# Dividing attention by its row sums behind the weighted sum of values instead of ahead of the transposes

## What is computed

```python
q = _rms_norm(q, g_q)
k = _rms_norm(k, g_k)
logits = jnp.einsum('bhqd,bhkd->bhqk', q, k) * d ** (-0.5)
attn = jax.nn.softmax(logits, axis=-1)
o = jnp.einsum('bhqk,bhkd->bhqd', attn, v)
o = jnp.swapaxes(o, 1, 2).reshape(b, n, dim)
return o + o @ W_out
```

## Time and profile before

| what | us |
|---|---|
| median of 3 runs | 3099.62 |
| the three runs | 3105.89, 3098.64, 3099.62 |
| the profiled execution, device time | 3095.6 |
| its span, first to last instruction | 3093.5 |
| start of batch 1 / batch 2 in it (first sum of squares on TensorE) | 186.03 / 292.83 |
| start of the last network, behind batch 7 | 961.5 |
| first matmul of layer 1 | 1039.5 |

### The profile page before, as it was taken

How to read it: one execution, slowest core, us unless ns; L and a number is a source line. 1 busy time by engine, 2 the same in 40 slices (tenths; PEclk the granted TensorE clock), 3 DMA queues, 4 the chain that set the end, 5 groups by cost and what they waited for, 6 DMA issues and landing times.

```text
span 3093.5 us, 130035 instructions
## 1 busy us (share of the span) xinstructions
PE 2879.0 (93%) x47184; PEld 2502.9 (81%) x47184; DVE 1746.1 (56%) x6459; ACT 1065.8 (34%) x4862; POOL 1284.5 (42%) x3409
## 2 busy tenths in 40 slices
PE   6899999999999556899999999999999999999998
PEld 4368777767778455899999899899899899899987
DVE  1636644644642444566666666666666666666654
ACT  1122332543442122333333333333333333333322
POOL 0000000100110466666666566566566566656600
PEclk7589999999999655799999999999999999999999
DMA  4613312532532000244444444444344444444466
GB/s 146 201 38 103 99 58 67 183 95 88 184 101 75 25 0 0 71 128 130 135 129 126 127 131 128 125 130 127 119 139 127 123 130 128 119 135 129 129 215 203
DMA packets 137146, 359.18 MB, mean 116 GB/s; under 512 B 16016, under 2 KB 24848, under 8 KB 136592
## 3 DMA queue, kind: packets, MB, share of 16 engines
q1 hardware_dynamic: 136336, 353.72, 37.7%
q10 hardware_dynamic: 672, 3.67, 0.3%
HBM read 322.85 MB, written 34.47 MB: 116 GB/s over the span
## 4 chain that ended last, share of the span: by engine, by line
PE 60%; DVE 3%; issue 2%; ACT 1%; DMA 0%; DVEq 0%; POOL 0%; ACTq 0%; SPq 0%; POOLq 0%
PE pscan L1019 13%; PE pscan L1015 13%; PE pg L946 11%; PE pd L972 11%; PE pu L946 11%; ACT th L869 1%; DVE state L1176 1%; DVE qraw L1176 0%; PE prouter L1029 0%; PE prouter L1037 0%; DMA wgu<-w_split 0%; PE pd L1044 0%; DVE pscan L1162 0%; DVEq L1175 0%; DVE th L1159 0%
## 5 line engine op out<-in xcount | busy, mean ns | idle before, releaser
L1015 PEld LDWEIGHTS pscan<-th,clo 128*128 128x128 f16 x16384 | 555.8, 97 | 143.5 <-ACT th L869 123.0
L1015 PE MATMUL pscan<-th,clo 128*128 128x8 f16 x16384 | 564.3, 167 | 109.8 <-ACT th L869 109.8
L1019 PE MATMUL pscan<-th,chi 128*128 128x16 f16 x16384 | 561.5, 170 | 3.0 <-DVE th L1159 2.3
L1019 PEld LDWEIGHTS pscan<-th,chi 128*128 128x128 f16 x16384 | 486.8, 97 | 4.5 <-DVE th L1159 4.5
L946 PE MATMUL pg<-qh,wgu 128*128 128x256 f16 x3168 | 430.5, 275 | 16.7 <-issue 15.8
L972 PE MATMUL pd<-hg,wd 128*128 128x256 f16 x3168 | 429.8, 275 | 2.2 <-DMA wd<-w_split 2.2
L946 PE MATMUL pu<-qh,wgu 128*128 128x256 f16 x3168 | 426.3, 274 | 0.0
L869 ACT ACTIVATE th<-state 128x32 f16<-128x32 f32 x768 | 175.9, 229 | 719.3 <-DVE state L1176 719.1
L1176 DVE TENSOR_REDUCE state<-pscan 128x32 f32<-128x96 f32 x768 | 197.4, 257 | 265.0 <-PE pscan L1019 259.7
L946 PEld LDWEIGHTS pg<-qh,wgu 128*128 128x128 f16 x3168 | 295.5, 98 | 55.9 <-issue 17.2
L946 PEld LDWEIGHTS pu<-qh,wgu 128*128 128x128 f16 x3168 | 294.1, 98 | 34.0
(11 more groups left out here) (164 smaller groups left out, 4286.8 us busy)
## 6 DMA issues: line engine op xcount, KB each, us to landing
wgu<-w_split SPq DMA_DIRECT2D x264, 512.0 KB, 3.6
wd<-w_split SPq DMA_DIRECT2D x264, 384.0 KB, 3.1
part_in<-in_w_tiles SPq DMA_DIRECT2D x120, 256.0 KB, 3.0
w_split<-part_out SPq DMA_DIRECT2D x99, 256.0 KB, 2.8
late<-in_w_tiles SPq DMA_DIRECT2D x78, 256.0 KB, 3.0
w_split<-late SPq DMA_DIRECT2D x33, 128.0 KB, 3.3
hid<-in_up_q SPq DMA_DIRECT2D x8, 512.0 KB, 4.0
hid<-in_up_s SPq DMA_DIRECT2D x16, 256.0 KB, 5.5
```

What stands on the lines that cost most here:

```text
L1015: mm(pscan[:, 0, m * B:(m + 1) * B], clo[:, k, m * P:(m + 1) * P], th[:, k, 0, :], start=(m == 0 and k == 0), stop=False, skip_group_check ...
L1019: ins = mm(pscan[:, 0:2, m * B:(m + 1) * B], chi[:, k, m * P:(m + 1) * P], th[:, k], start=False, stop=(k == NC - 1), skip_group_check=True)
```

## The change

The exponentials are transposed as they are. `normed` and the accumulated sums go away. In `weighted(c)` eight matmuls more, ahead of the eight with the values, multiply the same transposed exponentials `prT` with a 128x32 block of ones; they leave the sum of each query on the 32 rows of its head, in columns 256 to 511 of the same bank. On VectorE `inverse(c - 1)` takes the reciprocal of these 128x256 sums and `gathered(c - 1)` multiplies it into the weighted sums; both stand inside quad c, behind `turned(h + 1)` and `turned(h + 2)`, and those of quad 3 behind the loop. ScalarE no longer copies `Ob`.

```diff
@@ scalar
                         ins = act.activation(pr[:, h % HPC, qc, :], X[h % HPC][:, qc * T:(qc + 1) * T], ACT.Exp,
-                                             bias=nmax[:, h % HPC, qc:qc + 1], accum_out=psum_e[:, h, qc:qc + 1])
+                                             bias=nmax[:, h % HPC, qc:qc + 1])
-                def gathered(c):
-                    act.wait_ge(S["p_pv"], b * NC + c + 1)
-                    act.activation(oT[:, c, :], Ob[c % 2][:, 0:T], ACT.Copy).then_inc(S["a_oT"], 1)
@@ tensor
                 def transposed(h):
-                    pe.wait_ge(S["d_pn"], b * HEADS + h + 1)
+                    pe.wait_ge(S["a_exp"], b * HEADS + h + 1)
@@ tensor, weighted(c)
                     if c >= 2:
-                        pe.wait_ge(S["a_oT"], b * NC + c - 1)
+                        pe.wait_ge(S["d_oT"], b * NC + c - 1)
+                    for kc in range(2):
+                        for j in range(HPC):
+                            mm(Ob[c % 2][DH * j:DH * (j + 1), T:2 * T], ones[:, 0:DH], prT[:, j, kc, :], start=(kc == 0), stop=(kc == 1))
@@ vector
-                def normed(h):
-                    dve.wait_ge(S["a_exp"], b * HEADS + h + 1)
-                    dve.reciprocal(rinv[:, h, :], psum_e[:, h, :]).then_inc(S["d_rinv"], 1)
-                    dve.wait_ge(S["d_rinv"], b * HEADS + h + 1)
-                    for qc in range(2):
-                        ins = dve.tensor_scalar(pr[:, h % HPC, qc, :], pr[:, h % HPC, qc, :], rinv[:, h, qc:qc + 1], None, ALU.mult)
-                    ins.then_inc(S["d_pn"], 1)
+                def inverse(c):
+                    dve.wait_ge(S["p_pv"], b * NC + c + 1)
+                    dve.reciprocal(rinv, Ob[c % 2][:, T:2 * T]).then_inc(S["d_rinv"], 1)
+                def gathered(c):
+                    dve.wait_ge(S["d_rinv"], b * NC + c + 1)
+                    dve.tensor_tensor(oT[:, c, :], Ob[c % 2][:, 0:T], rinv, ALU.mult).then_inc(S["d_oT"], 1)
@@ vector, the loop over quads
                     row_max(h)
                     row_max(h + 1)
-                    normed(h)
                     row_max(h + 2)
-                    normed(h + 1)
                     turned(h)
                     row_max(h + 3)
-                    normed(h + 2)
                     turned(h + 1)
-                    normed(h + 3)
+                    if c:
+                        inverse(c - 1)
                     turned(h + 2)
+                    if c:
+                        gathered(c - 1)
                     turned(h + 3)
                     if ffn and c == NC - 1:
                         second(b - 1, 0)
+                inverse(NC - 1)
+                gathered(NC - 1)
```

More of the change, by code:

```diff
@@ L87, in layer0 @@
         nmax = sb("nmax", [P, HPC, 2])
-        psum_e = sb("psum_e", [P, HEADS, 2])
-        rinv = sb("rinv", [P, HEADS, 2])
+        rinv = rs[:, 0, :]
         late = sb("late", [P, N + H0 + NC * T])
@@ L108, in layer0 @@
                  "p_nrm p_qk p_hr p_v p_s p_t p_pv p_wo p_up p_dn "
-                 "a_sqx a_rstd a_sq a_hr a_v a_exp a_oT a_up "
-                 "d_xn d_qk d_max d_rinv d_pn d_pt d_x1 d_x2 "
+                 "a_sqx a_rstd a_sq a_hr a_v a_exp d_oT a_up "
+                 "d_xn d_qk d_max d_rinv d_pt d_x1 d_x2 "
                  "chain achain seq plseq "
@@ L315, in batch @@
                     exps(HPC * c + 1)
-                    if c:
-                        gathered(c - 1)
                     relus(ffn_quad[c][0:2])
@@ L322, in batch @@
                     relus(ffn_quad[c][3:])
-                gathered(NC - 1)
             batch(0, False)
@@ L466, in batch @@
                     pe.wait_ge(S["wo_in"], 16)
-                pe.wait_ge(S["a_oT"], b * NC + NC)
+                pe.wait_ge(S["d_oT"], b * NC + NC)
                 for m in range(NC):
@@ L591, in batch @@
                     if i == 0:
-                        dve.wait_ge(S["a_oT"], b * NC + NC)
+                        dve.wait_ge(S["d_oT"], b * NC + NC)
                     dve.tensor_tensor(x1[:, 2 * i:2 * i + 2, :].rearrange("p a t -> p (a t)"), Rb[i][:], oT[:, 2 * i:2 * i + 2, :].rearrange("p a t -> p (a t)"), ALU.add).then_inc(S["d_x1"], 1)
```

## The result

| | before | changed |
|---|---|---|
| median of 20 runs each, us | 3099.14 | 3104.72 |
| lowest and highest | 3092.95, 3105.89 | 3101.43, 3112.13 |
| profiled execution, device time | 3095.6 | 3109.9 |
| its span | 3093.5 | 3107.9 |

The ratio of changed to before is 1.002, with a 95% interval of 1.0014 to 1.0026: **slower by 5.6 us (4.3 to 8.1)**. The borders of the stages are good to 0.4 us.

A forecast was written before the change was run, and what follows sets the result against it. TensorE bounds batches 1 to 3, with waits in batches 4 to 7 and a half-clock ring in batch 0. 17.0 + 3.1 + 7.2 = 27.3 us, so about 3127 us, 0.9% slower; range 3108 to 3140.

The forecast's parts named there:

- one group of sums at full clock: Eight added matmuls with ones on TensorE: 0.86 us a group at full clock, 1.72 at half.
- the reciprocal: VectorE's 128x256 reciprocal from PSUM: 1.82 us, between bounds of 0.41 and 2.45.
- batches 1 to 3, a wait: TensorE waits 0.74 us for VectorE's row at the ends of quads 1, 2 and 3, 2.2 us a batch.
- batches 1 to 3, all: Sums of 3.44 us plus waits of 2.2 us lengthen each batch by 5.66 us: 17.0 us for three.
- batches 4 to 7: Sums outside quad 1 cost 10.3 us, waits for `normed` outside it give back 7.2: +3.1 us.
- batch 0, quad 0: First quad of batch 0, without sums: no gain or loss counted.
- batch 0, quads 1 and 2: `weighted` lies on the ring between `scores` and `lora`; sums at half clock cost 2 x 1.72 = 3.4 us.
- batch 0, quad 3 and the end: Nothing hides the last reciprocal and product; the projection begins 3.8 us later, at 181.0 instead of 177.19.
- the ReLU wait that stays: TensorE's wait for a ReLU behind the store ring, once in each of batches 4 to 7, remains at 2 us or more.
- What ScalarE loses ... and what VectorE loses gives nothing beyond the waits named: ScalarE's 256 accumulator reads and 32 copies, and VectorE's removed work, save nothing more: neither engine is waited for elsewhere.
- both give about the same time, so the ring and the ReLU stay: Quad 1, batches 4 to 7: `part_low` comes when it did, so the ReLU wait hides `weighted(0)`'s sum, costing nothing.
- the third: Rival, chance 0.09: store ring opens, ReLU wait goes, batches 4 to 7 14.1 us faster; 3110 us, narrow reciprocal 3100.

The follow-up runs named there:

- the first pair: Single profiled executions of the kernel before and the changed kernel, 3095.6 and 3109.9 us.
- the means: Averages of batches 4 to 7 over several traces: attention of the kernel before 457.9 us, of the changed kernel 455.7 us.
- the kernels of the first group: Here, kernel before with the eight sum matmuls added, result unused: in every quad 3121.37 us, in batch 0 only 3097.28 us.
- the new form: Attention as in the changed kernel, in all or some batches; the changed kernel took 3104.72 us, run again 3110.29.
- the ReLU first: Last ReLUs ahead of the store-waiting high parts in quad 1 of batches 4 to 7: kernel before 3081.43 us, changed kernel 3095.07 us.
- its later half: Changed kernel's attention in batches 1 to 7, that of the kernel before in batch 0: 3116.72 us, again 3113.34 us.
- the early reciprocal behind batch 0: Changed kernel with reciprocal and product ahead of a quad's first copy in batches 1 to 7 alone: 3104.67 us, ratio 1.0011.
- the early reciprocal everywhere: Changed kernel with reciprocal and product ahead of a quad's first copy in all batches: 3107.07 us, ratio 1.0025.
- the copy: Changed kernel with a plain copy of the 128x256 sums in place of the reciprocal: 3103.74 us, ratio 1.0006.
- the kernel with the sums alone: Kernel before with the eight matmuls with ones added in each quad, result unused: 3121.37 us, ratio 1.007.
- the frame: Both attention forms in one program with two unused tensors: changed kernel's form everywhere 3107.48 us, form of the kernel before everywhere 3101.98 us.
- The halves run apart: Kernel before with the changed attention in batch 0 alone, 3098.34 us; in batches 1 to 7 alone, 3116.72 and again 3113.34 us.
- the old form: Attention as in the kernel before, in all or some batches; the kernel before took 3099.14 us.

## The prediction against the runs, step by step

| step | forecast | measured |
|---|---|---|
| one group of sums at full clock | 0.86 | 0.87 |
| the reciprocal | 1.82 | 1.75 |
| batches 1 to 3, a wait | 3 x 0.74 a batch | 2 x 0.44 a batch |
| batches 1 to 3, all | +17.0 | +13.2 |
| batches 4 to 7 | +3.1 | +3.3 in the first pair, -2.2 in the means |
| batch 0, quad 0 | 0 | -1.7 in the first pair |
| batch 0, quads 1 and 2 | +3.4 | -2.6 in the first pair |
| batch 0, quad 3 and the end | +3.8 | +2.5 in the first pair |
| all | +27.3 | +5.6 |

**Right.** The sums at full clock, the reciprocal, the untouched layer 1, the ReLU wait that stays, and that no engine is spared anything that counts in batches 1 to 3.

**The waits for the reciprocal** were right in kind and too long. The rows above have 8.57 us for VectorE where I had 8.88, of which 0.16 is that the next instruction starts 1.66 us after a reciprocal begins and 0.08 the same for the product. A wait of 0.44 us stands only in quads 2 and 3; in quad 1 TensorE's own stretch is 0.49 us longer by a ReLU wait, which covers it. 3.47 + 2 x 0.44 = 4.35 us a batch of the 4.41 measured.

**Batch 0 is where the forecast failed most**, by some 10 of the 22 us, in two steps. First, "In quads 1 and 2 `weighted` lies between `scores` and `lora`, on the ring: 2 x 1.72 = 3.4 us". That the sums lie on the ring is right, but the step holds the granted clock at what it was. TensorE in the changed kernel:

```profile
93.02 3.78 PE L358 MATMUL l0bank<-late 16*128 16x512 f32 x4 [1.76 <-DVE w_up L508]
...
113.58 1.93 PE L437 MATMUL l0bank<-work,ones 128*32 128x256 f32 x16
115.28 1.14 PE L441 MATMUL l0bank<-work 128*32 128x256 f32 x16
116.35 1.98 PE L358 MATMUL l0bank<-late 16*128 16x512 f32 x4
119.71 1.98 PE L358 MATMUL l0bank<-late 16*128 16x512 f32 x4 [0.80 <-DVE w_dn L508]
123.43 3.77 PE L358 MATMUL l0bank<-late 16*128 16x512 f32 x4 [1.16 <-DVE w_dn L508]
```

From `weighted` to the end of the first `lora`, with the sums in it, it takes 116.35 + 1.98 - 113.58 = 4.75 us; without them in the kernel before 117.06 + 3.78 - 115.20 = 5.64 us. The clock rises within the 32 records (1.70 us for the first 16, 1.07 for the second) and holds through two `lora`. Quad 1 by the windows, before and after:

```profile
113.18:138.28 25.10, 23.16 (x64) 9.30 (x65) 17.50 (x32) 4.25 (x17) 0.00 (x0) 0.50 0.57 167
111.56:134.35 22.79, 19.57 (x81) 8.37 (x81) 16.74 (x22) 3.13 (x8) 0.00 (x0) 0.65 0.68 184
```

That the sums bring the price down to nothing in quads 1 and 2 is shown by the kernels of the first group. Why the quad with two `lora` at full clock appears only with the new form (quad 1 in some traces, quad 2 in others) is not shown; without any sum the first `lora` of quad 2 ran faster as well in some traces, at 2.31 us in the new form and 2.22 in the old. Second, the sentence "What ScalarE loses ... and what VectorE loses gives nothing beyond the waits named" is wrong for quad 0, which has no sums: it is 1.7 us shorter (24.32 for 26.04), as its second `lora` waits 1.76 us for VectorE (93.02 above) instead of 3.19. The end of the batch is there as forecast, but smaller:

```profile
169.79 1.70 PE L437 MATMUL l0bank<-work,ones 128*32 128x256 f32 x16 [2.20 <-DVE work L566]
171.25 1.95 PE L441 MATMUL l0bank<-work 128*32 128x256 f32 x16
173.25 1.76 DVE L558 RECIPROCAL rs<-l0bank 128x256 f32<-128x256 f32 x1 [3.51 <-PE l0bank L441]
...
175.61 8.83 PE L466 MATMUL l0bank<-late,w_out 128*128 128x256 f32 x32 [2.41 <-DVE late L561]
```

The projection waits 2.41 us for the exposed reciprocal and product, where the earlier trace rows has 0.59. It starts 1.6 us earlier than in the kernel before, not 7 us later.

**Batches 4 to 7** have the waits nearly as forecast, and one error in the account. The forecast took the sum of quad 1 as hidden by the ReLU wait, and gave back 7.2 of the 10.9 us of waits for `normed`. All of them went, and the ReLU wait grew by 1.6. Waits and sums alone make +13.8 - 10.9 + 1.6 = 4.5 us; by the full-clock stretch of 4 x 106.80 = 427.2 us, of which about 2 us is a ReLU wait too, the changed kernel should take 427.2 + 13.8 + 12.2 - 2 = 451.2 us, which its traces at clock 1.00 show (451.0). The kernel before should take 446.7, and no trace of it does: 455 to 459, at clock 0.98 or 0.99. Of these 8 us some 5 were lost clock: TensorE is busy for 428.94 us in the kernel before and for 423.67 with the ReLU first, where the clock is full. The other 3 are there with the ReLU first as well (439.56 us, where the same sum gives 427.2 + 11.3 - 2 = 436.5), and what they are is open. The step that failed is "both give about the same time, so the ring and the ReLU stay": they stay, but the clock behind them does not have to, and with the new form it is 1.00 in two of five traces of the full change or its later half. That the change brings this about, and not chance, is not shown. The kernel with the early reciprocal behind batch 0 has 451.2 us as well, but those with the early reciprocal everywhere and with the copy have 457.4 and 458.7.

**The sum in two halves.** My steps give the sums alone 10.3 + 10.3 + 6.9 = 27.5 us and everything else about nothing. Measured as whole kernels, the sums alone are +21.6 us, and the rest of the change takes 21.6 - 5.6 = 16 us back. Both halves were forecast too high. The stages show only 10 of the 16 us: between the kernel with the sums alone and the mean of the new form they are -0.6 us in batch 0, +2.9 in batches 1 to 3 and -12.5 in batches 4 to 7, where 10.1 us of waits for `normed` go.

**Of the rivals**, the third had the nearest times, 3110 and 3100, by a mechanism that did not occur: its ReLU wait goes, here it is 12.2 us. None had batch 0 shorter, and the rise of the clock by work that is added was not among them.

**What stays open.** The stage means give -2.5 + 13.2 - 2.2 = +8.5 us, the medians +5.6, +8.6 and, in the frame, +5.8. The halves run apart give -2.6 with +15.8 or +11.7, so 9 to 13 us, which is more than the whole. A stretch that the change does not touch, from the start to the first scores of batch 0, varies from 85.1 to 90.1 us in these profiled executions, and layer 1 from 2052 to 2060 us, so differences of some 4 us can't be given to one stage from single traces. What decides whether the clock holds behind a wait of 2 to 3 us was not found.

## What to carry to other kernels

Before pricing an added matmul in a stretch with a granted clock well below 1, ask what the clock does once it is added: here 1.72 us of matmuls at half clock came out at nothing in quads 1 and 2, while the same work at full clock cost its full 0.86 us. A normalization moved from many narrow operations to one wide one needs a place in the order with slack behind it: in batches 1 to 3 the reciprocal of 1.75 us cost 1 us a batch ahead of the last two copies and nothing ahead of the first, and in batch 0 the early place cost 4 us. And a wait that ends late for another reason hides what a change does: with the ReLU ahead of the store ring the change costs 13.6 us, not 5.6.

## What the runs showed of the hardware

Matmuls added to batch 0, which runs mostly at half clock, raised its granted clock from 0.57 or 0.58 to between 0.63 and 0.66, with the old form and with the new. In the old form they paid for themselves in quads 1 and 2 (24.7 to 25.0 us with them, 24.7 to 25.1 without); in quad 3 they cost 1.0 us in the old form and 2.0 in the new, of 3.4 us added. The same program with the same waits (12.1 and 12.2 us) ran batches 4 to 7 in 451.0 us at clock 1.00 and in 458.3 us at 0.98. The clock fell behind a wait of 2.00 us and held behind one of 3.22. A reciprocal of 256 elements a partition from PSUM took 1.75 us, and the next VectorE instruction began 1.66 us after it; a product of the same size took 0.41 us and let the next begin after 0.33.
